# Edge keys by rounding, rounds on GpSimd, features turned ahead of the keys, and a basis schedule two parts later

## The chip, the cores and the metric

The kernel runs on one core of a Trainium2 chip. The metric is device microseconds (us) for one execution, median of several runs. All times below are us unless marked ns.

## The reference

Two graph layers over 625 nodes with 512 features each and 20,625 edges (`src`, `dst`, and a type of 0 or 1):

- Layer 0: `xw = x @ W.T`; with `deg` the number of edges into a node and `dinv = deg ** -0.5`, `h = dinv * (A @ (dinv * xw)) + b`, where `A` counts the edges between two nodes, the node itself included. Then batch norm over the nodes, gelu, `+ x`, and layer norm of `x + h`.
- Layer 1: two passes of a gated relational layer. `w[r] = sum_b att[r, b] * basis[b]` for two relations and 30 bases of 512x512; a message is `sigmoid(x[col] . gate_w[r]) * x[col] @ w[r]`, summed over the edges of type `r` into a node, plus `x @ root + bias`. Relu after the first pass, then `layernorm(x + out)`.

The two times 30 bases are 63 MB of float32 that must be read from memory.

## The kernel before

**Basis stream.** The bases are read in 64 parts of 1 MB, numbered 0 to 63, into a ring of four buffers (`basis_ring`, L397) by the SyncE queue. Part n is issued when part n-4 has been used by TensorE (`basis_used`). A part is used by 16 matmuls of 128x512 (L515); four parts sum up in one PSUM bank, and eight parts make one block of `w`. `basis_upto(n)` in TensorE's program uses the parts up to n, two at a time, and is called at fixed places.

**Edge counts.** The counts of edges between nodes, for each type, are built in `B` from 27 groups of six columns of 128 sorted edges. For a group, VectorE writes two one-hot tiles (`oh_src` and `oh_key`, L1088), TensorE multiplies them into PSUM (L596), and VectorE adds two windows of 16 nodes to `B` at an offset that it reads into a register (`window_at`, L1071, `add_window`, L1081), two groups behind. Ahead of the loop, the edges are turned by TensorE and the keys computed on VectorE. The number of further rounds (none, if every window is narrow enough) is computed by `rounds()` at group 12 and read into a register behind the loop, as are the last four window offsets.

**Beside the loop**, TensorE turns `x` (five transposes of four blocks) and `W` (four), computes `xw` in 20 steps (L563), and uses basis parts. VectorE merges the first eight parts at group 13 (`w_merge`) and writes their low halves at group 15 (`w_low`).

**Behind the loop**: the sums of the two types give `AT` (L1155, some of them turned to float by ScalarE, L846), TensorE computes `deg` (25 matmuls of two columns, L619), GpSimd the inverse root, both scale `xw` to `z`, and TensorE aggregates in four steps `f` (L639), with the counts turned to `BB` in between (L651). GpSimd issues 16 transfers of `root1` here (L455). After the gelu, TensorE turns the result back (L677), and all that follows hangs on that.

The order is written out by hand for each engine. TensorE's basis schedule in the stretch that matters is: `basis_upto(min(3 * g // 4 - 1, 17))` in group g; `basis_upto(19)` ahead of `deg`; 21 behind it; 23 after the first aggregation; 25, 27, 27 after f = 1, 2, 3; 31 ahead of the transposes of L677.

Of the kernel before, what the change touches and what calls it, by code (L numbers as in the profile page):

```python
# [38 lines left out]
P = 128  # L39
N = 625  # L40
# [18 lines left out]
MAXW = -(-N // W)  # L59
# [16 lines left out]
SWAPPED = [i ^ 1 for i in range(32)]  # L76


def gnn_block(nc, x, src, dst, etype, W0, b0, gamma, beta,
# [28 lines left out]
    with ctx:  # L108
# [50 lines left out]
        gmm = sb("gmm", [1, 4, NW], F32)  # L159
        base_i = sb("base_i", [1, NW], I32)  # L160
        spans = sb("spans", [1, MAXW], F32)
# [27 lines left out]
        edges_in, att_in = sem("edges_in"), sem("att_in")  # L189
# [44 lines left out]
        uses, releaser = {}, []  # L234

# [4 lines left out]
        for a in range(3):  # L240
            use(("edge", a), "dve")
        use("minmax", "dve")

        use("base", "dve")
        turned = [("xT", 0), ("xT", 1)] + [("w0T", k) for k in range(KC)] + [("xT", c) for c in range(2, NC)]
        use("att", "dve")
        for name in turned:
            use(name, "act")
# [101 lines left out]
        FIRST_IN = 23  # L350
# [20 lines left out]
        def edge_rows(eng, a, v):  # L371

            whole = E // (2 * P)
            eng.dma_start(rows_i[0:whole, a], v[0:whole * 2 * P].rearrange("(t h e) -> t h e", h=2, e=P)) \
                .then_inc(edges_in, 16)
            eng.dma_start(rows_i[whole:ROWS, a].rearrange("t h e -> t (h e)")[:, 0:E - whole * 2 * P],
                          v[whole * 2 * P:E].rearrange("(t e) -> t e", t=1)).then_inc(edges_in, 16)
# [5 lines left out]
        def _(sp):  # L383
            sp.wait_ge(rows_set, 3)
            edge_rows(sp, 1, dst)
# [28 lines left out]
        def _(pool):  # L414
# [20 lines left out]

            pool.wait_ge(consts, 5)
            pool.wait_ge(vec_in, 16 * 6)
# [53 lines left out]
        def _(pe):  # L491
# [38 lines left out]
            pe.wait_ge(rows_ready, 1)  # L530
            for a in range(3):
                wait_free(pe, ("edge", a))
                for h in range(2):
                    last[0] = nc.tensor.transpose(bank(("edge", a))[:, h * ROWS:(h + 1) * ROWS], rows_f[:, a, h, :],
                                                  ident[0:ROWS, 0:ROWS])
                done()
            pe.wait_ge(minmax_ready, 1)
# [3 lines left out]
            done()  # L541
            def turn(i):
# [13 lines left out]
            def xw_part(i):  # L556
# [3 lines left out]
                pe.wait_ge(in_turned, 3 + k if c == 0 else 1 + KC + c)  # L560
# [9 lines left out]
            done()  # L570
            pe.wait_ge(att_in, 16 * 2)
            pe.wait_ge(spread_ready, SUB)
# [14 lines left out]
            for i in range(FIRST_TURNS):  # L587
                turn(i)
            for g in range(NG):
# [39 lines left out]
            basis_upto(21)  # L629
# [149 lines left out]
        def _(act):  # L779
            act.wait_ge(rows_set, 3)  # L780
            edge_rows(act, 0, src)
            edge_rows(act, 2, etype)
# [34 lines left out]

            act.wait_ge(consts, 4)
            counts = B[:].rearrange("p s t n -> p (s t n)").bitcast(F32)
            link(nc.scalar.activation(counts, ones_f[0:PC, 0:1].broadcast_to(list(counts.shape)), ACT.Copy, scale=0.0))  # L820
# [132 lines left out]
        def _(dve):  # L953
# [15 lines left out]
            for q in range(SUB):  # L969
                v.tensor_copy(spread[:, q * P:(q + 1) * P].rearrange("p (b k) -> p b k", k=KB),  # L970
                              ident[0:NB, bases(q)].unsqueeze(2).broadcast_to([NB, BG, KB])).then_inc(spread_ready, 1)
            dve.wait_ge(edges_in, 16 * 6)
            link(v.tensor_copy(rows_f[:], rows_i[:]))
# [368 lines left out]
```

## Time and profile before

| what | value |
|---|---|
| runs | 312.93, 314.32, 317.32 us; median 314.32 |
| profiled execution, own time | 314.59 us |
| its span, first to last instruction | 312.7 us |
| mean granted TensorE clock | 0.960 of full |
| TensorE / VectorE / ScalarE / GpSimd busy | 88% / 51% / 29% / 12% |
| read from memory | 72.05 MB |

The span is the time between the first and the last instruction of the profiled execution; the own time is what that execution took as a whole.

### The profile page before, as it was taken

The page shows a single profiled execution, that of the slowest core. Times are in us where ns is not written, and L with a number is a line of the kernel's source. Part 1 is how long each engine was busy: PE and PEld are TensorE (multiplying, and loading weights), DVE is VectorE, ACT ScalarE, POOL GpSimd, SP SyncE. Part 2 cuts the span into 40 slices and gives each one's busy share as a digit, 9 for nine tenths or more (in the row PEclk, how much of TensorE's full clock was granted, in tenths as well). Part 3 has the DMA queues.
Part 4 walks back from the last instruction along what each step waited for, and adds up shares of the span by engine and source line. Part 5 has one row for each costly group of instructions (what it writes and reads, how often), then busy time and mean ns, then how long its engine had stood idle before and what let it go on. Part 6 is the DMA issues. An engine that isn't in the chain of part 4 may idle for free.

```text
span 312.7 us, 4598 instructions
## 1 busy us (share of the span) xinstructions
PE 276.0 (88%) x1687; PEld 180.8 (58%) x1687; DVE 160.3 (51%) x362; ACT 89.5 (29%) x140; POOL 38.3 (12%) x73
## 2 busy tenths in 40 slices
PE   1589958989799977679999999999997999999991
PEld 1573413433566643237765656677774878787770
DVE  3888888884656856855221241342434225334443
ACT  5160220201436876551352104112212242100000
POOL 2001000000292106500000000000005500011111
PEclk9999986999779999779999999999999999999997
DMA  6998992999989999958994897976002400001112
GB/s 164 231 418 326 353 410 80 415 375 369 364 259 307 413 398 426 371 183 299 388 379 171 366 343 283 419 286 265 21 1 52 118 0 0 0 2 33 33 33 66
DMA packets 12802, 73.63 MB, mean 235 GB/s; under 512 B 2000, under 2 KB 2243, under 8 KB 4588
## 3 DMA queue, kind: packets, MB, share of 16 engines
q1 hardware_dynamic: 11330, 70.82, 60.7%
q0 software_dynamic: 1104, 2.36, 2.9%
q8 instruction: 13, 0.21, 0.3%
q10 hardware_dynamic: 346, 0.17, 0.2%
q14 instruction: 9, 0.07, 0.1%
HBM read 72.05 MB, written 1.28 MB: 235 GB/s over the span
## 4 chain that ended last, share of the span: by engine, by line
PE 62%; DVE 16%; DMA 8%; issue 7%; DVEq 3%; ACT 1%; POOL 1%; ACTq 0%; POOLq 0%
PE psW L515 15%; PE psM L496 9%; PE psM L497 8%; PE psM L498 8%; PE psM L753 7%; DMA basis_ring<-in_L_gnn_basis_dram 7%; PE psM L773 6%; DVE B L1081 4%; DVEq L1071 2%; PE psM L563 2%; DVE oh_key L1088 2%; PE psE L596 2%; DVE oh_src L1088 2%; DMA rows_i<-in_edge_type_dram 1%; PE psM L639 1%
## 5 line engine op out<-in xcount | busy, mean ns | idle before, releaser
L515 PE MATMUL psW<-basis_ring,S 128*32 128x512 f32 x512 | 67.9, 646 | 6.3 <-DVEq L1057 3.7
L1267 DVE SCALAR_TENSOR_TENSOR zg<-psM,gate,zg 125x512 fp32r<-125x512 f32 x20 | 15.0, 751 | 56.9 <-ACT zg L929 56.9
L515 PEld LDWEIGHTS psW<-basis_ring,S 128*32 128x32 f32 x512 | 13.5, 114 | 41.2 <-issue 27.4
L496 PE MATMUL psM<-w,hlT 128*125 128x512 f32 x80 | 32.4, 405 | 0.1
L498 PE MATMUL psM<-w,hlT 128*125 128x512 f32 x80 | 31.7, 396 | 0.0
L497 PE MATMUL psM<-w,hlT 128*125 128x512 f32 x80 | 31.7, 396 | 0.0
L929 ACT ACTIVATE zg<-psM,gate 125x512 fp32r<-125x512 f32 x20 | 13.8, 688 | 46.3 <-PE psM L498 45.9
L596 PEld LDWEIGHTS psE<-oh_key,oh_src 128*125 128x125 f16 x162 | 13.9, 143 | 22.4 <-issue 17.3
L753 PEld LDWEIGHTS psM<-BB,zg 125*128 125x128 f32 x160 | 23.1, 188 | 3.4 <-issue 2.5
L753 PE MATMUL psM<-BB,zg 125*128 125x320 f32 (+1 forms) x160 | 24.1, 309 | 0.0
L773 PE MATMUL psM<-zg,BB 125*125 125x512 f32 x100 | 24.0, 394 | 0.0
L1081 DVE TENSOR_TENSOR B<-B,psE 125x160 f32 x54 | 17.5, 324 | 11.1 <-issue 6.6
L596 PE MATMUL psE<-oh_key,oh_src 128*125 128x160 f16 x162 | 17.0, 245 | 6.9 <-DVE B L1081 6.8
L563 PE MATMUL psM<-w0T,xT 128*125 128x512 f32 x40 | 21.7, 634 | 0.0
L773 PEld LDWEIGHTS psM<-zg,BB 125*125 125x125 f32 x100 | 18.6, 186 | 4.7
L480 POOL DMA_DIRECT2D root_raw<-in_L_gnn_root_dram x16 | 7.9, 501 | 106.8 <-DVE hlT L1297 106.8
L496 PEld LDWEIGHTS psM<-w,hlT 128*125 128x125 f32 x80 | 14.8, 185 | 9.0 <-issue 2.5
L1088 DVE TENSOR_TENSOR oh_key<-iota_f,key_pairs 128x960 f16<-128x960 f16 x27 | 17.7, 654 | 0.3
L498 PEld LDWEIGHTS psM<-w,hlT 128*125 128x125 f32 x80 | 14.8, 185 | 3.8
L497 PEld LDWEIGHTS psM<-w,hlT 128*125 128x125 f32 x80 | 14.8, 185 | 3.4
L1067 DVE TENSOR_TENSOR w<-w_both,w 128x512 fp32r<-128x512 f32 x16 | 13.1, 861 | 7.1 <-ACT w L816 6.5
L800 ACT ACTIVATE w_half<-psW,mask_h 128x512 f32<-128x512 f32 x16 | 10.1, 679 | 20.0 <-PE psW L515 20.0
(154 smaller groups left out, 381.0 us busy)
## 6 DMA issues: line engine op xcount, KB each, us to landing
basis_ring<-in_L_gnn_basis_dram SPq DMA_DIRECT2D x64, 1024.0 KB, 7.3
root_raw<-in_L_gnn_root_dram POOLq DMA_DIRECT2D x32, 64.0 KB, 3.6
xs<-in_x_dram SPq DMA_DIRECT2D x1, 1120.0 KB
out_dram<-xs SPq DMA_DIRECT2D x5, 224.0 KB
w_raw<-in_L_gnn_W_dram SPq DMA_DIRECT2D x4, 256.0 KB, 9.6
bias_b<-in_L_gnn_bias_dram POOLq DMA_DIRECT2D x1, 250.0 KB, 3.5
xs<-in_x_dram SPq DMA_DIRECT2D x1, 130.0 KB
out_dram<-xs SPq DMA_DIRECT2D x5, 26.0 KB
```

The source lines that it names most:

```text
L496: nc.tensor.matmul(o, l_hi, r_hi, start=start, stop=False)
L497: nc.tensor.matmul(o, l_hi, r_lo, start=False, stop=False)
L498: last[0] = nc.tensor.matmul(o, l_lo, r_hi, start=False, stop=stop)
L515: m = nc.tensor.matmul(psW[32 * j:32 * j + 32, cc % 2, :], S[:, cc % 2, cc // CH, q].rearrange("p k r -> p (k r)"), ring[:, n % RING, j, : ...
L563: last[0] = nc.tensor.matmul(bank(("xw", c))[0:PC, :], xT[:, k, n], w0T[:, k], start=(k == 0), stop=(k == KC - 1))
L596: nc.tensor.matmul(psE[0:PC, g % 2, at:at + KEYS], oh_src[:, g % 3, j * P:j * P + PC], oh_key[:, t % OH, :], start=(j % SG == 0), stop=(j ...
L753: last[0] = nc.tensor.matmul(bank(("h", f, h))[:, 0:n], zg[:, i, d, r, f * P:(f + 1) * P], BB[:, at:at + n], start=(d + r + i == 0), stop= ...
L773: last[0] = nc.tensor.matmul(bank(("out", c))[0:PC, :], BB[:, at:at + PC], zg[:, i, d, r, :], start=False, stop=(d == NC - 1 and r + i == 2))
L929: nc.scalar.activation(zg[:, 0, c, r, :], bank(("Z", L, c, r))[0:PC, :], ACT.Copy, scale=gate[:, L, c, r:r + 1]).then_inc(zg_hi, 1)
L1081: v.tensor_tensor(to, to, psE[0:PC, g % 2, h * KEYS:(h + 1) * KEYS] .rearrange("p (c t w) -> p c t w", c=NC, t=R), ALU.add).then_inc(win_a ...
L1088: return v.tensor_tensor(out, pair.unsqueeze(1).broadcast_to(shape), pairs[:, first:first + n].unsqueeze(2).broadcast_to(shape), ALU.is_equal)
L1267: link(v.scalar_tensor_tensor(out=zg[:, 1, c, r, :], in0=bank(("Z", L, c, r))[0:PC, :], scalar=gate[:, L, c, r:r + 1], in1=zg[:, 0, c, r, ...
```

## The change

- The keys: the chunk of a source (`src // 125`) is found by scaling, adding and subtracting a large number, instead of four comparisons; copies into `edgeT` and `base_b` are left out, VectorE reads PSUM instead; the type and chunk terms are scaled by 1/1024, so that one fused instruction brings the penalty for edges beyond a window.
- The edges: three semaphores instead of one. VectorE casts only `dst`; ScalarE casts `src` and the types and copies the turned `dst`. Clearing `B` moves from ScalarE to GpSimd. TensorE turns `dst` first, then the minima and maxima, then the other two.
- `rounds()` goes from VectorE at group 12 to GpSimd ahead of the loop, in 11 small linked instructions.
- All five turns of `x` come ahead of the loop (two of them ahead of the `att` matmuls), the four of `W` at groups 2 and 3; `xw` comes one group earlier.
- `S` is built in four instructions instead of eight and a memset.
- The first merge is at group 17 instead of 13, the low halves at 19 instead of 15.
- The registers of the last four windows and of the rounds are read between the two sums of groups 23 to 26 and 14, instead of behind the loop.
- The basis schedule: `7 * g // 10 - 2` in group g (so up to part 15 in the loop); 17 inside `deg`, behind its tenth matmul; 19 behind the vectors; 21 after the first aggregation; 23, 27, 27 after f = 1, 2, 3; 31 as before.

```diff
-        turned = [("xT", 0), ("xT", 1)] + [("w0T", k) for k in range(KC)] + [("xT", c) for c in range(2, NC)]
+        turned = [("xT", c) for c in range(NC)] + [("w0T", k) for k in range(KC)]
-        FIRST_IN = 23
+        FIRST_IN = 21
-        PARTS_IN = 17
-        FIRST_TURNS = 3
-        TURN_AT = {0: (3,), 1: (4, 5), 2: (6, 7), 3: (8,)}
-        ROUNDS_AT = 12
-        MERGE_AT = {13: 0}
-        LOW_AT = {15: 0}
+        TURN_AT = {2: (NC, NC + 1), 3: (NC + 2, NC + 3)}
+        MERGE_AT = {17: 0}
+        MORE_AT = 14
+        LOW_AT = {19: 0}
...
+            counts = B[:].rearrange("p s t n -> p (s t n)").bitcast(F32)
+            nc.gpsimd.memset(counts, 0.0).then_inc(b_clear, 1)
             pool.wait_ge(consts, 5)
+            pool.wait_ge(base_ready, 1)
+            link(nc.gpsimd.tensor_tensor(gmm[0:1, 2, :], gmm[0:1, 1, :], gmm[0:1, 0, :], ALU.subtract))
+            link(nc.gpsimd.tensor_scalar(gmm[0:1, 2, :], gmm[0:1, 2, :], -(W - 1) / 2.0, 1.0 / W, ALU.add, ALU.mult))
+            link(nc.gpsimd.tensor_scalar(gmm[0:1, 2, :], gmm[0:1, 2, :], ROUNDING, ROUNDING, ALU.add, ALU.subtract))
+            n = NW
+            while n > 1:
+                link(nc.gpsimd.tensor_tensor(gmm[0:1, 2, 0:n // 2], gmm[0:1, 2, 0:n // 2], gmm[0:1, 2, n - n // 2:n], ALU.add))
+                n -= n // 2
+            link(nc.gpsimd.tensor_scalar(more_f[:], gmm[0:1, 2, 0:1], float(N // W), None, ALU.min))
+            nc.gpsimd.tensor_copy(more_i[:], more_f[:]).then_inc(rounds_ready, 1)
...
+            for i in range(AHEAD_OF_ATT):
+                turn(i)
             pe.wait_ge(att_in, 16 * 2)
...
-                xw_upto(3 * (g - 2) // 4)
-                basis_upto(min(3 * g // 4 - 1, PARTS_IN))
+                xw_upto(3 * (g - 1) // 4)
+                basis_upto(7 * g // 10 - 2)
...
-            basis_upto(19)
             wait_free(pe, "deg")
...
+                if s == AT_ORDER[1]:
+                    basis_upto(17)
...
-            basis_upto(21)
+            basis_upto(19)
...
+            for a, arrived in ((0, src_in), (2, etype_in)):
+                act.wait_ge(arrived, 16 * 2)
+                nc.scalar.activation(rows_f[:, a], rows_i[:, a], ACT.Copy).then_inc(side_rows, 1)
+            wait_full(act, "dst")
+            link(nc.scalar.activation(edgeT[:, 1, :], bank("dst")[:, 0:T], ACT.Copy))
...
-            link(v.tensor_scalar(chunk[:], edgeT[:, 0, :], float(PC), None, ALU.is_ge))
-            for c in range(2, NC):
-                link(v.scalar_tensor_tensor(out=chunk[:], in0=edgeT[:, 0, :], scalar=float(c * PC), in1=chunk[:],
-                                            op0=ALU.is_ge, op1=ALU.add))
+            link(v.tensor_scalar(chunk[:], bank("src")[:, 0:T], -float(PC // 2), 1.0 / PC, ALU.add, ALU.mult))
+            link(v.tensor_scalar(chunk[:], chunk[:], ROUNDING, ROUNDING, ALU.add, ALU.subtract))
...
                 for i, w in enumerate(range(2 * (g - 2), 2 * (g - 1)) if g >= 2 else ()):
                     add_window(w, at[i])
-                if g == ROUNDS_AT:
-                    rounds()
+                    if i == 0 and g == MORE_AT:
+                        dve.wait_ge(rounds_ready, 1)
+                        more = nc.values_load(more_i[0:1, 0:1], engines=[mybir.EngineType.DVE], min_val=0, max_val=N // W)
+                    if i == 0 and g >= NG - 4:
+                        late.append(window_at(NW - NG + g))
...
-            more = nc.values_load(more_i[0:1, 0:1], engines=[mybir.EngineType.DVE], min_val=0, max_val=N // W)
-            at = [window_at(w) for w in range(NW - 4, NW)]
```

## Rows read from the trace of the kernel before

**Rows 1.** The page: busy time by engine; DMA share in 40 slices of 7.8 us

```profile
PE 276.0 (88%) x1687; PEld 180.8 (58%) x1687; DVE 160.3 (51%) x362; ACT 89.5 (29%) x140; POOL 38.3 (12%) x73
...
DMA  6998992999989999958994897976002400001112
```

**Rows 2.** Chain that ended last, 90 to 120 us: start, us, what

```profile
95.63 12.10 DMA basis_ring<-in_L_gnn_basis_dram
...
108.90 8.77 DMA basis_ring<-in_L_gnn_basis_dram
...
118.78 0.65 PE psM L677 x4
```

**Rows 3.** Issues of parts 12, 20 and 31, each with its time to landing

```profile
L397 SPq DMA_DIRECT2D basis_ring<-in_L_gnn_basis_dram x1: 328/328/328, 52.6 to 52.6; - x1
DMA to landing us min/median/max: 4.8/4.8/4.8
...
L397 SPq DMA_DIRECT2D basis_ring<-in_L_gnn_basis_dram x1: 328/328/328, 72.4 to 72.4; - x1
DMA to landing us min/median/max: 8.7/8.7/8.7
...
L397 SPq DMA_DIRECT2D basis_ring<-in_L_gnn_basis_dram x1: 327/327/327, 108.9 to 108.9; - x1
DMA to landing us min/median/max: 8.8/8.8/8.8
```

**Rows 4.** Busy time in three windows; last three columns: granted clock, DMA share, GB/s

```profile
76.00:78.00 2.00, 2.00 (x8) 0.53 (x10) 0.97 (x3) 0.30 (x1) 0.00 (x0) 1.00 0.97 410
...
86.00:88.00 2.00, 2.00 (x12) 0.39 (x8) 2.00 (x3) 2.00 (x4) 2.00 (x3) 0.50 0.50 201
88.00:90.00 2.00, 2.00 (x12) 0.71 (x5) 2.00 (x4) 0.15 (x1) 2.00 (x6) 0.59 0.77 209
```

**Rows 5.** Timeline, 0 to 22 us: start, us, engine line operation

```profile
6.14 0.56 DVE L973 CAST rows_f<-rows_i 81x768 f32<-81x768 int32 x1 [2.28 <-DMA rows_i<-in_edge_type_dram]
...
12.36 1.86 PE L575 MATMUL psM<-att_t,w_half 30*128 30x4 f32 x8 [2.01 <-DMA att_t<-in_L_gnn_att_dram]
...
14.13 0.55 DVE L1088 TENSOR_TENSOR oh_src<-iota_f,place_pairs 128x756 f16<-128x756 f16 x1
...
15.27 1.12 DVE L1022 TENSOR_TENSOR S<-mask_k,psM 128x64 f32<-128x64 f32 x8
...
16.72 1.01 PE L596 MATMUL psE<-oh_key,oh_src 128*125 128x160 f16 x6
...
16.90 0.55 DVE L1088 TENSOR_TENSOR oh_src<-iota_f,place_pairs 128x756 f16<-128x756 f16 x1
```

**Rows 6.** Timeline of VectorE: the rounds' first instruction, and what follows their last

```profile
39.96 0.20 DVE L1030 TENSOR_TENSOR gmm<-gmm 1x54 f32<-1x54 f32 x1
...
41.08 0.55 DVE L1088 TENSOR_TENSOR oh_src<-iota_f,place_pairs 128x756 f16<-128x756 f16 x1
```

**Rows 7.** Chain that ended last, end of the loop: sums and register loads

```profile
73.31 0.32 DVE B L1081
...
73.97 0.30 DVEq L1071
...
74.30 0.19 DVEq L1071
...
76.60 0.33 DVE B L1081
...
77.06 0.34 DVE B L1081
...
77.59 0.33 DVE B L1081
```

**Rows 8.** Timeline of TensorE behind the loop: `deg`, then parts 20 and 21

```profile
80.40 3.15 PE L619 MATMUL psM<-ones_r,AT 125*125 125x2 f32 x25 [0.69 <-ACT AT L846]
...
85.72 3.64 PE L515 MATMUL psW<-basis_ring,S 128*32 128x512 f32 x16 [1.65 <-DVEq L1057]
```

More of the change, by code:

```diff
@@ L234, in gnn_block @@
         uses, releaser = {}, []
+        AHEAD_OF_ATT = 2
         def use(name, by):
@@ L238, in use @@
             releaser.append(by)
-        for a in range(3):
-            use(("edge", a), "dve")
+        use("dst", "act")
         use("minmax", "dve")
+        use("src", "dve")
+        use("etype", "dve")
         use("base", "dve")
-        turned = [("xT", 0), ("xT", 1)] + [("w0T", k) for k in range(KC)] + [("xT", c) for c in range(2, NC)]
+        turned = [("xT", c) for c in range(NC)] + [("w0T", k) for k in range(KC)]
+        for name in turned[:AHEAD_OF_ATT]:
+            use(name, "act")
         use("att", "dve")
-        for name in turned:
+        for name in turned[AHEAD_OF_ATT:]:
             use(name, "act")
@@ L384, in _ @@
             sp.wait_ge(rows_set, 3)
-            edge_rows(sp, 1, dst)
+            edge_rows(sp, 1, dst, dst_in)
             for p in (slice(0, WIDE), slice(WIDE, PC)):
@@ L529, in _, with edges_turned @@
             pe.wait_ge(consts, 4)
-            pe.wait_ge(rows_ready, 1)
-            for a in range(3):
-                wait_free(pe, ("edge", a))
+            def edges_turned(name, a):
+                wait_free(pe, name)
                 for h in range(2):
-                    last[0] = nc.tensor.transpose(bank(("edge", a))[:, h * ROWS:(h + 1) * ROWS], rows_f[:, a, h, :],
+                    last[0] = nc.tensor.transpose(bank(name)[:, h:T:2], rows_f[:, a, h, :],
                                                   ident[0:ROWS, 0:ROWS])
                 done()
+            pe.wait_ge(rows_ready, 1)
+            edges_turned("dst", 1)
             pe.wait_ge(minmax_ready, 1)
@@ L585, in xw_upto @@
                 steps_done[0] = max(steps_done[0], n)
-            for i in range(FIRST_TURNS):
+            for i in range(AHEAD_OF_ATT, NC):
                 turn(i)
@@ L977, in _ @@
             last.then_inc(minmax_ready, 1)
-            for a in range(3):
-                wait_full(dve, ("edge", a))
-                to, ps = (ap.rearrange(how, h=2) for ap, how in ((edgeT[:, a, :], "p (t h) -> p h t"),
-                                                                 (bank(("edge", a))[:, 0:T], "p (h t) -> p h t")))
-                link(v.tensor_copy(to, ps) if a < 2 else
-                     v.tensor_scalar(to, ps, 0.0, float(W), ALU.not_equal, ALU.mult))
-                dve.sem_inc(free_dve, 1)
             wait_full(dve, "minmax")
@@ L1019, in build_S @@
                 att = bank("att")[:, 0:2 * R * SUB].rearrange("p (q l r) -> p l q r", q=SUB, l=2)
+                shape = [P, 2, SUB, KB]
                 for i, r in itertools.product(range(2), range(R)):
-                    for l in range(2):
-                        last = v.tensor_tensor(S[:, i, l, :, :, r], mask_k[:].unsqueeze(1).broadcast_to([P, SUB, KB]),
-                                               att[:, l, :, (i + r) % R].unsqueeze(2).broadcast_to([P, SUB, KB]), ALU.mult)
+                    last = v.tensor_tensor(S[:, i, :, :, :, r], mask_k[:].unsqueeze(1).unsqueeze(1).broadcast_to(shape),
+                                           att[:, :, :, (i + r) % R].unsqueeze(3).broadcast_to(shape), ALU.mult)
                 link(last)
                 dve.sem_inc(free_dve, 1)
-                link(v.memset(S[0:own(SUB - 1) * KB, :, :, SUB - 1], 0.0))
                 dve.sem_inc(ident_in, 1)
-            def rounds():
-                link(v.tensor_tensor(gmm[0:1, 2, :], gmm[0:1, 1, :], gmm[0:1, 0, :], ALU.subtract))
-                link(v.tensor_reduce(gmm[0:1, 3, 0:1], gmm[0:1, 2, :], AX.X, ALU.max))
-                link(v.tensor_scalar(spans[:], iota_f[0:1, 1:MAXW + 1], float(W), gmm[0:1, 3, 0:1], ALU.mult, ALU.is_le))
-                link(v.tensor_reduce(more_f[:], spans[:], AX.X, ALU.add))
-                link(v.tensor_copy(more_i[:], more_f[:]))
             def w_merge(pp):
@@ L1089, in one_hots @@
                                        pairs[:, first:first + n].unsqueeze(2).broadcast_to(shape), ALU.is_equal)
+            late = []
             for g in range(NG):
```

79 lines of the change are left out of this document (49 added, 30 removed).

## The prediction

> **What bounds the kernel now.** I read the page first. TensorE is busy for 88% of the span, but the DMA slices are full as well from the start to about 215 us [rows 1]: two resources are near their limit, and the busy shares alone don't say which one a given stretch hangs on. The change touches nothing behind L677 (the transposes after the gelu), so the question is which wait ends last ahead of it. The chain of waits answers it: it runs through the transfer of a basis part from 95.63 for 12.10 us, and again from 108.90 for 8.77 us, and then straight into L677 at 118.78 [rows 2]. The start of L677 therefore hangs on the landing of part 31, not on VectorE's loop. Behind L677 the same code runs in the same order, so I take it that whatever L677 moves by, the end moves by.
>
> The issues then show what limits the landing of part 31. The SyncE queue issues parts in order, each when the part four before it has been used. On an idle queue a part lands after 4.8 us (part 12, 52.6) [rows 3]. With others in front it takes 8 to 12 us: part 20 (72.4) lands at 81.1, part 31 (108.9) at 117.7 [rows 3]. At full speed the queue moves 410 GB/s [rows 4], so a part of 1.05 MB costs 2.56. Between the landings of parts 20 and 31 lie 36.6 us for 11 parts, of which 28.1 are the parts themselves. The other 8.5 are the 16 transfers of `root1`, which share the engines, and a gap: at 86 to 90 the DMA share is 0.50 and 0.77, which is 1.0 + 0.5 = 1.5 us not used [rows 4]. So from part 20 on the queue runs almost without a break, and the landing of part 31 is the landing of part 20 plus a nearly fixed time.
>
> **The change part by part.** First the loop, where it should save time.
>
> Start. Ahead of the keys VectorE casts one array instead of three, waits for `dst` only, and drops several linked instructions of some 0.3 each; first one-hots start at 14.13 now [rows 5], and I expect 11 to 12. But group 1 waits for `S`, and `S` for the `att` matmuls, which start at 12.36 when their data land and take 1.86 [rows 5]. Nothing in the change brings that transfer forward. `S` is then built from 14.2, in about 0.9 instead of 1.12 and a memset, and group 1 starts at 15.2 instead of 16.90 [rows 5]: 1.7 gained. TensorE still has three turns between `att` and the matmuls of group 0, which stay at 16.72 and take 1.01 [rows 5]; VectorE wants their sum two groups on, at 15.2 + 2 x 1.14 (14.13 to 15.27 is one pair of one-hots [rows 5]) = 17.5, and waits some 0.4. I take 1.2. The bounds: 1.7 if TensorE keeps up; 0.3 if `x` lands so late that its first two turns hold up `att` behind them on TensorE (no row shows its landing). The extra work on ScalarE (three small copies) and GpSimd (clearing `B`, 11 small instructions) ends long before anything needs it; VectorE needs the cleared `B` only at its first sum, and the rounds at group 14. Without that cover the rounds would cost VectorE a wait at group 14, with all later groups behind it.
>
> Rounds. Their five instructions on VectorE go: 39.96 to 41.08 is 1.1 [rows 6], and a little of TensorE's starvation behind them, 0.2. The merges move, with the same instructions; TensorE starves at group 17 instead of 13, which costs nothing as VectorE sets the pace there.
>
> Registers. Behind the loop the next to last sums wait for five register reads: 73.31 to 76.60 instead of the usual 0.53 between two sums of different groups (77.06 to 77.59) [rows 7]. That saves 2.8. One read is 0.30 plus 0.19 and gaps, 0.62 in all (3.1 for five). Between two sums it starts beside the first one and lets the second start 0.72 later instead of 0.46 (76.60 to 77.06) [rows 7]: 0.26 each, 1.3 for five. Bounds: 0.16 and 0.62 each.
>
> Sum: 1.2 + 1.1 + 0.2 + 2.8 - 1.3 = 4.0 us. `deg` starts at 76.4 instead of 80.40 [rows 8]. TensorE has fewer parts to use in the loop and should be free by then.
>
> The rule for the register read speaks against this part. The Trainium skill, page "DMA: Bandwidth & Descriptors", section "Latency and other measured facts", gives about 600 ns as the floor of a `tensor_load`. The trace agrees with that for the whole read (0.62), but not for the load alone (0.30). By the rule as it stands, nothing of it would be hidden, and five reads would cost 3.1; that is a rival below.
>
> Now the basis schedule. Parts 16 and 17 were used in the loop; now they stand inside `deg`, behind its tenth matmul. 10 of 25 matmuls of a stretch of 3.15 [rows 8] take 1.3, so they start at 77.7. Two parts took 3.64 at a granted clock of 0.50 [rows 4, 8], so 1.8 at full clock and 0.9 each: part 16 is used up at 78.6. Only then is part 20 issued, on a queue that has just run dry (parts 18 and 19 follow the use of 14 and 15, near 72), and it lands at 78.6 + 4.8 = 83.4. Before it landed at 81.1. So here the queue is 2.3 us later, although the loop is 4.0 earlier. The steps behind (19, 21, 23 instead of 21, 23, 25) are also one pair behind, but their parts are used early enough to keep the queue full: 22 and 23 are issued near 83, `root1` near 85, 24 and 25 near 91. With that work outstanding the gap of 1.5 at 86 to 90 is filled. Part 31 lands at 83.4 + 36.6 - 1.5 = 118.5 if all of the gap is filled, and at 120.0 if none is: 0.8 to 2.3 later than now. I take 1.3, since part of what looked like a gap is latency that stays.
>
> TensorE's side of `deg` costs nothing more: `deg` is 1.8 longer by the parts in it, but the 3.64 of parts 20 and 21 and the 1.65 of waiting ahead of them [rows 8] leave the path to the first aggregation.
>
> Where VectorE's and TensorE's 4 us go, then, is into longer waits for basis parts, at f = 2 (parts 26 and 27, now used there in a row with 24 and 25) and ahead of L677.
>
> Sum: the profiled execution had 314.59 us, 1.9 more than its span, and 0.27 more than the median of 314.32. 314.32 + 1.3 = 315.6.
>
> **The rivals.**
> (a) The queue is not the limit, and the gain of the loop reaches L677. For it: parts could land closer together than now, since `root1` comes at another point against them; the 8.5 us that they lose now is the largest unknown in my sum. Against it: the chain of waits names the transfers twice [rows 2], and the ring allows four parts ahead, no more. The compute side alone would start L677 about 3.4 earlier (4.0, less part of the time by which the last gelu is held up by four parts in a row ahead of f = 3). It gives 314.3 - 3.4 = 310.9.
> (b) Slower: TensorE has nothing to do for one or two us ahead of `deg`, and then matmuls of two columns. In the trace its granted clock is at 0.50 in 86 to 88, behind just such a stretch (a wait, `deg`, and a wait of 1.65) [rows 4, 8]. If it falls about 5 us earlier against the work, parts 16 and 17 take 1.8 each. Part 20 lands 0.9 later; if besides the start has gained 0.3 and not 1.2, another 0.9; and if the gap isn't filled, 2.3 instead of 1.3. Together 4.1: 318.4. It decides when part 20 lands after 84.5.
> (c) The register reads hide nothing (the rule above): the loop ends 5 x 0.36 = 1.8 later than in my sum, and so does part 20: 317.4.
> (d) The start doesn't gain at all, as `att` or `x` lands later: 1.2 more, 316.8. This is inside the range.
>
> **How the numbers follow.** Forecast, the queue sets L677 and lands 0 to 3 later: 0.50. (a) 0.27; (b) 0.12; (c) and (d) together 0.06; 0.05 for what I haven't seen. The range leaves out the ends of (a) and (b): from 310.9, the whole price of (a), to 318.6, that of (b). 2% is 6.3 us, which is about what a measurement of this kernel can tell from no change (its runs lie 4.4 us apart). Neither (a) nor (b) reaches it. Faster by over 2% needs the whole gain of 4.0, and 2.3 more; slower needs (b) and further lost clock behind it. I give 0.07 to each side, one more hundredth to slower.
>
> **What would show it right or wrong.** Right: `deg` starts at 75.5 to 77.5; no register reads behind the last groups; part 20 is issued at 78 to 80 and lands at 83 to 85; parts 20 to 31 land within 35 to 37 us; the chain of waits still goes through a basis transfer into L677, which starts at 119 to 121; TensorE waits longer for basis parts between 100 and 120 than it does now. Wrong: L677 starts before 117; the chain ahead of it goes through the gelu or VectorE's statistics instead of a transfer; `deg` starts after 79 (the loop's terms fail); parts 24 to 27 land without the delay from `root1`; or the end moves by something else than L677 does, as TensorE's granted clock falls at other places behind it.

## The result, and the profile after

The changed kernel takes 318.94 us (median of 4 runs, 316.86 to 321.30), the kernel before 315.82 us beside it (4 runs, 312.93 to 317.56). The ratio is 1.013, with a 95% interval of 1.008 to 1.019: slower by a little over one per cent, and outside the range that I gave by 0.3 us. My forecast of 315.6 was built on 314.32 for the kernel before, so 1.5 of the 3.3 us between 315.6 and 318.94 lie in that base (it measured 315.82 here, and 313.70 to 314.43 in three later sets of runs) and not in the change. The profiled execution of the changed kernel took 317.14 us with a span of 315.3.

The page reads almost as before [rows 1]: TensorE 88%, VectorE a little less, GpSimd 5.8 us more.

```profile
PE 278.3 (88%) x1687; PEld 183.3 (58%) x1687; DVE 159.1 (50%) x345; ACT 87.6 (28%) x142; POOL 44.1 (14%) x85
...
DMA  6994999397889999987994977977101400001112
```

The chain of waits (the work that ended last, each piece with what released it) runs from the end of the loop to the transposes behind the gelu (L707 now). It has the same two transfers in it as before [rows 2]. Each row is start, duration, what.

```profile
76.44 0.60 ACT xw L868
77.03 0.62 ACT AT L882
...
77.79 1.22 PE psM L646 x10
79.02 2.42 PE psW L533 x16
81.44 3.24 PE psM L646 x15
84.68 0.53 PE psM L655 x4
85.20 3.57 PE psW L533 x16
88.78 3.84 PE psM L669 x20
...
100.73 1.90 PE psW L533 x16
...
102.64 9.29 DMA basis_ring<-in_L_gnn_basis_dram
...
111.98 1.11 PE psW L533 x8
...
113.11 8.77 DMA basis_ring<-in_L_gnn_basis_dram
...
121.92 1.07 PE psW L533 x8
122.99 0.65 PE psM L707 x4
```

The transposes start at 122.99 instead of 118.78: 4.2 later, with a transfer of a basis part straight ahead of them as before. The first transfer in the chain is part 27. It is issued when part 23 has been used, at 102.64 instead of 95.63 [rows 2]. That is 7.0 later, of which its transfer gives back 2.8 (9.29 instead of 12.10); the last step, part 31, takes 8.77 in both.

Between 77.79 and 102.64 no transfer stands in the chain: it is TensorE's own order of work, with a short piece on ScalarE and VectorE at 93.5 to 96.4. In the kernel before it is the same, in the same chain as [rows 2] and [rows 7]:

```profile
80.40 3.17 PE psM L619 x25
...
85.72 3.64 PE psW L515 x16
89.36 3.24 PE psM L639 x20
92.60 1.11 PE psM L661 x10
93.72 1.90 PE psW L515 x16
```

Behind the first aggregation both kernels stand level. A pair of parts starts at 93.65 in the kernel before and at 93.66 in the changed one. But before it is the pair 22 and 23, and now it is 20 and 21; the pair 22 and 23 comes behind the next aggregation, at 100.66. That is the 7.0 us. The 2.6 us by which the loop ends earlier have gone by then into parts 16 to 19, which now all stand behind it.

The issues on the SyncE queue, here of parts 20 and 31, give the other end of that stretch:

```profile
L401 SPq DMA_DIRECT2D basis_ring<-in_L_gnn_basis_dram x1: 327/327/327, 80.1 to 80.1; - x1
...
DMA to landing us min/median/max: 4.8/4.8/4.8
...
L401 SPq DMA_DIRECT2D basis_ring<-in_L_gnn_basis_dram x1: 327/327/327, 113.1 to 113.1; - x1
...
DMA to landing us min/median/max: 8.8/8.8/8.8
```

Part 20 lands at 84.9 (81.1 before [rows 3]) and part 31 at 121.9: 37.0 between them, where 36.6 lay before. Part 20 isn't waited for in either kernel: it is used from 85.72 before and from 93.66 now, 4.6 and 8.8 us behind its landing.

TensorE around `deg` shows what happens in between (start, duration, operation; in brackets the idle time ahead of it and what ended that):

```profile
77.79 1.22 PE L646 MATMUL psM<-ones_r,AT 125*125 125x2 f32 x10 [1.39 <-ACT AT L882]
78.94 2.50 PE L533 MATMUL psW<-basis_ring,S 128*32 128x512 f32 x16
81.37 3.31 PE L646 MATMUL psM<-ones_r,AT 125*125 125x2 f32 x15
...
85.13 3.64 PE L533 MATMUL psW<-basis_ring,S 128*32 128x512 f32 x16
```

Parts 16 and 17 take 2.50, 15 of the `deg` matmuls 3.31, parts 18 and 19 3.64. The windows of the same stretch (granted clock, DMA share and GB/s last) say why:

```profile
78.00:80.00 2.00, 2.00 (x22) 1.34 (x25) 1.20 (x2) 0.87 (x2) 0.00 (x0) 1.00 0.89 377
80.00:82.00 2.00, 2.00 (x13) 0.63 (x4) 0.00 (x0) 0.00 (x0) 0.00 (x0) 0.54 0.49 111
82.00:84.00 2.00, 2.00 (x11) 2.00 (x11) 0.00 (x0) 0.00 (x0) 0.00 (x0) 0.50 1.03 418
...
86.00:88.00 2.00, 2.00 (x16) 0.38 (x8) 1.68 (x2) 1.79 (x4) 1.92 (x3) 0.50 0.59 246
```

The mean granted clock is 0.54 in 80 to 82 and 0.50, the 1.2 GHz level, from then on: it fell inside `deg`. And the queue is still not full: its share is 0.49 at 80 to 82 and 0.59 at 86 to 88. The gap that I wanted filled has moved, and there are two.

### The profile page after: what moved, and what is told of

Read it like the earlier page. It is cut to its first block, busy times and chain, and to the rows that moved or that the text cites. A ratio compares the mean times of both kernels' runs of the same rounds, so it can differ in the third digit from the quotient of the medians.

```text
span 315.3 us, 4596 instructions
## 1 busy us (share of the span) xinstructions
PE 278.3 (88%) x1687; PEld 183.3 (58%) x1687; DVE 159.1 (50%) x345; ACT 87.6 (28%) x142; POOL 44.1 (14%) x85
## 4 chain that ended last, share of the span: by engine, by line
PE 67%; DVE 13%; DMA 8%; issue 6%; DVEq 3%; ACT 1%; POOL 1%; SPq 0%; POOLq 0%; ACTq 0%
PE psW L533 14%; PE psM L514 9%; PE psM L516 8%; PE psM L515 8%; PE psM L783 8%; PE psM L803 6%; DMA basis_ring<-in_L_gnn_basis_dram 6%; DVE B L1106 4%; DMA xs<-in_x_dram 3%; PE psM L588 2%; PE psM L669 2%; DVE oh_key L1113 2%; DVEq L1096 2%; PE psE L623 2%; PE psM L574 1%
## 5 line engine op out<-in xcount | busy, mean ns | idle before, releaser
L533 PE MATMUL psW<-basis_ring,S 128*32 128x512 f32 x512 | 66.5, 636 | 7.0 <-DMA basis_ring<-in_L_gnn_basis_dram 4.8
L846 ACT ACTIVATE w<-w_both 128x512 fp32r<-128x512 f32 x16 | 12.9, 847 | 12.5 <-DVE w_both L1073 11.7
```

The lines of the kernel that those rows point to most:

```text
L533: m = nc.tensor.matmul(psW[32 * j:32 * j + 32, cc % 2, :], S[:, cc % 2, cc // CH, q].rearrange("p k r -> p (k r)"), ring[:, n % RING, j, : ...
```

## The experiments

Twelve kernels ran. Absolute medians differ from one set of runs to the next, so each verdict is the ratio to the kernel before, measured beside it, with its 95% interval. The ratios near one per cent have overlapping intervals; what tells those apart is the place of the events in the trace. I collect both here; times are in us, "part 23 used" is the issue of part 27, and the last column is the start of the transposes behind the gelu, by TensorE's timeline (the chain has it 0.07 later). Places are good to 0.1 us and come from one profiled execution of each kernel.

```
kernel                     ratio to before        part 20  part 23  part 31  transposes
                                                  lands    used     lands    start
before                     1                      81.1     95.6     117.7    118.7
after                      1.013 (1.008 to 1.019)  84.9    102.6    121.9    122.9
e1 old basis order         0.989 (0.984 to 0.994)  75.9     93.7    114.6    115.6
e2 new basis order alone   1.037 (1.031 to 1.043)  96.3    113.8    131.6    132.6
e3 four parts before deg   1.007 (1.003 to 1.010)  84.0     97.6    119.0    120.0
e4 four parts inside deg   1.011 (1.007 to 1.015)  84.6     96.0    119.7    120.8
e5 new order, late merge   1.021 (1.013 to 1.029)  89.2    106.5    126.0    127.0
e6 old order, early merge  0.986 (0.981 to 0.991)  76.6     94.1    113.9    115.9
e7 wide deg matmuls        1.009 (1.005 to 1.012)  84.9    101.4    120.1    121.1
e8 root1 not read          1.006 (1.002 to 1.010)  85.1    102.9    120.9    122.8
e9 22, 23 earlier          1.008 (1.003 to 1.012)  85.1     98.0    120.2    121.3
e10 e6 with wide deg       0.987 (0.984 to 0.991)  77.2     93.2    114.7    115.8
e11 e6, registers behind   0.990 (0.986 to 0.993)  76.6     93.5    114.2    115.2
e12 e6, clear on ScalarE   0.991 (0.987 to 0.995)  76.9     92.7    114.0    115.1
```

**Is it the basis schedule?** e1 is the changed kernel with the schedule of before put back, and nothing else.

```diff
-        FIRST_IN = 21
+        FIRST_IN = 23
...
-                basis_upto(7 * g // 10 - 2)
+                basis_upto(min(3 * g // 4 - 1, 17))
...
+            basis_upto(19)
...
-                if s == AT_ORDER[1]:
-                    basis_upto(17)
...
-            basis_upto(19)
-
+            basis_upto(21)
```

> The changed kernel with the basis schedule of the kernel before (up to part 17 in the loop, 19 ahead of deg, 21, 23, 25 behind it); keys, rounds, turns, merges and registers as changed. Theory Q (the transfers' queue ran dry because parts 16 to 19 are used later): part 20 is issued near 71 again, L677's transposes start at 116 to 118.5, and the time is 311 to 314, faster than the kernel before by 0.5 to 3. Rival C (the granted clock that falls inside deg is the cause, whatever the schedule): it still falls, the time stays at 317 or more. Rival L (the new loop and keys are slower): 317 or more, as nothing of them is taken back.

Measured: 310.63 us, ratio 0.989. `deg` starts at 78.12, no earlier than in the changed kernel, but parts 16 and 17 have been used in the loop, so part 20 is issued at 71.2 and lands at 75.9, 9.0 earlier, and the transposes start 7.3 earlier. The only difference between a kernel slower than before and one faster than before is this schedule. It is the cause of the loss.

e2 is the opposite: the kernel before with the new schedule alone (the same lines the other way round).

> The kernel before with the changed basis schedule alone. Theory Q: its loop ends about 2.6 later than that of the changed kernel, so part 20 is issued at 82 to 83, the transposes behind the gelu start at 124 to 126, and the time is 319 to 322, slower than the changed kernel. Rival C: as slow as the changed kernel only if the clock falls inside deg. Rival L: as the kernel before, 313 to 315.

Measured: 326.25 us, ratio 1.037, more than I expected. The reason is a collision that the changed kernel doesn't have. VectorE's timeline at the merge of before (group 13):

```profile
50.48 0.75 DVE L1049 SCALAR_TENSOR_TENSOR w_both<-psW,mask_h,w_half 128x512 f32<-128x512 f32 x1 [3.63 <-PE psW L515]
```

The merge needs parts 6 and 7, which the new schedule uses later, so VectorE stands still for 3.63 and the loop with it. (`deg` starts at 88.35, 6.8 later than in e5 below, so this wait isn't all of it; I didn't follow the rest.) Here the edit says more than the question asked. e5 therefore moves the merges along with the schedule:

```diff
-        MERGE_AT = {13: 0}
-        LOW_AT = {15: 0}
+        MERGE_AT = {17: 0}
+        LOW_AT = {19: 0}
```

> The kernel before with the changed basis schedule and the first merge at group 17 and its low halves at 19, as the changed kernel has them. Theory Q: VectorE no longer waits 3.6 us at group 13 for parts 6 and 7; deg starts near 81, part 20 is issued near 83 and lands near 88, the transposes behind the gelu start 36 to 38 later, near 125, and the time is 318.5 to 322. Rival M (the second pair of basis parts costs nothing by itself, and the 12 us of the run with the schedule alone came from the merge): 313 to 316, as the kernel before.

Measured: 321.23 us, ratio 1.021 (1.013 to 1.029). Part 20 lands at 89.2 instead of 81.1, and the transposes start 8.3 later. So the schedule by itself costs about 2%, and the changed kernel, at 1.013, has the loop's savings against it (the two intervals overlap). The later merge isn't an improvement by itself; it is what the later schedule needs.

**Where must the four late parts stand?** e3 uses parts 16 to 19 behind the loop, ahead of `deg`; e4 uses all four inside `deg`. Behind that both use the parts where the kernel before does (21, then 23 at `FIRST_IN`).

```diff
-        FIRST_IN = 21      # both
+        FIRST_IN = 23
...
+            basis_upto(19)      # e3: ahead of deg
...
-                if s == AT_ORDER[1]:      # e3: nothing inside deg
-                    basis_upto(17)
...
-                    basis_upto(17)      # e4: inside deg
+                    basis_upto(19)
...
-            basis_upto(19)      # both
-
+            basis_upto(21)
```

> The changed kernel, up to part 15 in the loop as changed, but parts 16 to 19 all used behind the loop ahead of deg, then 21, 23, 25 as in the kernel before. Theory Q: part 20 is issued near 77.3 instead of 80.1 and 22 near 79 instead of 87, so the transposes start 2 to 3.5 earlier than in the changed kernel although deg starts 2 later: 313.5 to 316. Rival C: deg's matmuls are in one stretch again; the clock falls at about 83 as in the kernel before: near 315. Rival L: 317 or more.

> The changed kernel with parts 18 and 19 used inside deg, right behind 16 and 17, then 21, 23, 25. Theory Q: part 20 is issued at 80.1 as in the changed kernel, 22 near 83 instead of 87.1, deg ends 2 to 3 later; the transposes start 1 to 2.5 earlier than in the changed kernel: 315 to 317.5. Rival C: the clock falls inside deg as now, and deg is longer: 317 to 319.

Measured: 1.007 and 1.011. Part 20 is issued at 77.7 and 79.9 and lands at 84.0 and 84.6, so the transposes come at 120.0 and 120.8. Both gain 2 to 3 us on the changed kernel's 122.9 and neither comes near e1's 115.6. e3's 316.59 us is 0.6 above what I had expected at most. What e1 has and e3 doesn't is the old schedule inside the loop, which has parts 16 and 17 in it (and the earlier parts two or three groups sooner). So of the 7.3 us by which the transposes differ between e1 and the changed kernel, 4.4 belong to the schedule inside the loop and 2.9 to the order behind it. In e3 `deg` starts at 82.35, and TensorE waits 2.01 for part 19 ahead of it; in e1, with the two parts used beside VectorE's loop, it starts at 78.12.

**Is it the gaps, the clock, or `root1`?** e7 tries to take the fall of the clock out of the changed kernel: the `deg` matmuls write 100 equal columns instead of 2, with the same count and the same result.

```diff
-                    last[0] = nc.tensor.matmul(bank("deg")[0:PC, 2 * c:2 * c + 2], AT[:, s, c * PC:(c + 1) * PC],
-                                               ones_r[:, 0:2], start=(s == AT_ORDER[0] and c == 0),
+                    last[0] = nc.tensor.matmul(bank("deg")[0:PC, 100 * c:100 * c + 100], AT[:, s, c * PC:(c + 1) * PC],
+                                               ones_r[:, 0:100], start=(s == AT_ORDER[0] and c == 0),
...
-            link(v.tensor_copy(deg[:], bank("deg")[0:PC, 0:2 * NC:2]))
+            link(v.tensor_copy(deg[:], bank("deg")[0:PC, 0:100 * NC:100]))
```

> The changed kernel; the 25 matmuls of deg stream 100 equal columns instead of 2. The weight load takes 0.12 of each matmul either way. Rival C (the granted clock that falls inside deg makes most of the 4 us): the clock stays at full through deg, parts 16 to 19 take 1.85 a pair, the transposes start 3 to 4 earlier and the time is 313.5 to 315.5. Theory Q: the clock accounts for the smaller share, 0.6 of the landing of part 20 and some 3 of the issue of part 22; if it stays up the transposes start 1 to 2 earlier, 315.5 to 317.5; if it falls nonetheless, 317 to 321 as now.

Its windows and TensorE's timeline:

```profile
80.00:82.00 2.00, 2.00 (x22) 1.16 (x15) 0.00 (x0) 0.00 (x0) 0.00 (x0) 1.00 0.47 102
82.00:84.00 2.00, 2.00 (x23) 1.32 (x26) 0.96 (x4) 0.38 (x2) 0.84 (x2) 1.00 0.96 406
```

```profile
80.88 1.84 PE L646 MATMUL psM<-ones_r,AT 125*125 125x100 f32 x15
...
82.99 1.92 PE L533 MATMUL psW<-basis_ring,S 128*32 128x512 f32 x16
```

The 15 `deg` matmuls take 1.84 instead of 3.31 and parts 18 and 19 1.92 instead of 3.64. Part 20 lands at 84.9 in both, but parts 22 and 23 are issued at 84.1 and 85.0 instead of 87.1 and 88.8. Part 31 lands at 120.1, which is 35.2 behind part 20 instead of 37.0. So the clock inside `deg` is worth 1.8 us of the 4.2. By the chain the gain is TensorE's: its first aggregation starts at 86.73 instead of 88.70, and part 23 is used at 101.4 instead of 102.6. In time the ratio goes from 1.013 to 1.009, with overlapping intervals.

e8 leaves out the transfers of `root1`: a clearing on GpSimd stands in for the 16 of them, so `root1` counts as zero in its product.

```diff
-                for j in range(JB):
-                    pool.dma_start(root1_raw[32 * j:32 * j + 32, kc],
-                                   root1.rearrange("(k c j) o -> c j k o", k=2 * KB, c=KC)[kc, j]) \
-                        .then_inc(root1_in, 16)
+                nc.gpsimd.memset(root1_raw[:, kc], 0.0).then_inc(root1_in, 1)
...
-            act.wait_ge(root1_in, 16 * KC * JB)
+            act.wait_ge(root1_in, KC)
```

> The changed kernel without the 16 transfers of root1: the tile is cleared by GpSimd instead, so root1's product is left out. It prices what these transfers take from the queue of the basis parts. Theory Q with the 8.5 us of the prediction put down to root1: parts 20 to 31 land within 29 to 32 us instead of 37, the transposes start 4 to 6 earlier, 312 to 315. Rival G (the time is lost in gaps of a queue that runs dry, root1 costs its 1 MB and no more): parts 20 to 31 take 34 to 36, the transposes start 1 to 3 earlier, 315 to 318.

Measured: 1.006 (1.002 to 1.010), part 31 35.8 behind part 20. With `root1` gone entirely only 1.2 us come back at part 31, and at the transposes 0.1, because part 31 is used at a lower clock in this profile (1.91 us instead of 1.07). I had laid a large part of 8.5 us on these transfers. But 1.2 isn't their price on the queue. Part 25 lands at 102.3 in e8 and at 107.0 in the changed kernel, 4.7 us apart; TensorE comes to it at 107.8 and 107.5, so in neither is it waited for. With `root1` gone the queue stands idle instead (its share is 0.40 at 94 to 96 and 0.54 at 102 to 104, where the changed kernel has 1.03 and 1.04), since the next parts are issued only when older ones have been used. What `root1` costs in the kernel before, where part 25 is used as it lands (101.5) and part 27's transfer in the chain takes 12.10, I didn't measure.

e9 changes one number of the changed kernel, `FIRST_IN` from 21 to 23, so that parts 22 and 23 are used right behind 20 and 21, after the first aggregation.

> The changed kernel with one number changed: 23 instead of 21 behind the first aggregation (so parts 20 to 23 are used there, 24 and 25 after f = 1, 26 and 27 after f = 2; 17 inside deg and 19 behind the vectors stay). Theory S (the delay is that of a chain: part 23 used, then the landing of part 27, then that of part 31): part 27 is issued near 97 to 98 instead of 102.6, its landing no longer waits for a late issue, the transposes behind the gelu start 2 to 4 earlier, and the time is 314.5 to 317. Theory Q as in the prediction (the queue is full from part 20 on, landings are fixed by part 20): part 31 lands at 121 to 122 as in the changed kernel and nothing is gained, 317.5 to 320.

Measured: 1.008, transposes at 121.3, 1.7 earlier. At first sight the later place of parts 22 and 23 costs 1.7. But in this profile the 15 `deg` matmuls ran at full clock (1.80) although they have two columns, so it must be read beside e7, not beside the changed kernel. Part 23 is then used 3.4 earlier (98.0 against 101.4), and part 31 lands at 120.2 against 120.1: nothing gained. TensorE now waits for the queue there, 1.13 for part 23 and 1.30 for part 25. So in the changed kernel the two limits, TensorE's order and the queue, lie close together. It also takes back a part of e7: two columns don't always let the clock fall there, so e7 shows what a full clock gives and not that the columns alone hold it.

**Is there a better kernel?** e6 is e1 with the merges back at groups 13 and 15; the other three change one thing in e6.

```diff
-        MERGE_AT = {17: 0}
+        MERGE_AT = {13: 0}
...
-        LOW_AT = {19: 0}
+        LOW_AT = {15: 0}
```

> The changed kernel with the basis schedule of the kernel before, and the merge at 13 and the low halves at 15 as well. Theory Q: parts 6 and 7 are used at group 11 in this schedule, so the place of the merge doesn't matter: 310 to 312, within 1 us of the same kernel with the merge at 17. Rival M (moving the merge is worth something by itself): over 2 us slower than that kernel.

Measured: 310.15 us, ratio 0.986 (0.981 to 0.991), the fastest here together with e10 (309.87 us, 0.987) and faster than both given kernels. Against e1 (0.989) there is no difference to be measured, so with the old schedule the place of the merge doesn't matter. Its chain of waits ahead of the transposes (L705 here) is of another kind:

```profile
113.82 1.26 ACT w_half L828 x2
115.08 0.80 ACT hf L912
...
115.93 0.72 PE psM L705 x4
```

Part 31 lands at 113.9 (TensorE waits 0.50 for it), and no transfer ends the wait ahead of the transposes: the gelu on ScalarE does, which stands in ScalarE's order behind four copies of weights. That holds for this profile only, and by under 1 us: in e1, e10, e11 and e12 the transfer of part 31 is again what TensorE waits for last ahead of the transposes, for 1.39 to 1.56 us.

e10 adds the wide `deg` matmuls of e7, e11 reads the five registers behind the loop as before, and e12 clears `B` on ScalarE instead of GpSimd:

```diff
-                    if i == 0 and g == MORE_AT:      # e11, in the loop
-                        dve.wait_ge(rounds_ready, 1)
-                        more = nc.values_load(more_i[0:1, 0:1], engines=[mybir.EngineType.DVE], min_val=0, max_val=N // W)
-                    if i == 0 and g >= NG - 4:
-                        late.append(window_at(NW - NG + g))
...
+            dve.wait_ge(rounds_ready, 1)      # e11, behind the loop
+            more = nc.values_load(more_i[0:1, 0:1], engines=[mybir.EngineType.DVE], min_val=0, max_val=N // W)
+            late = [window_at(w) for w in range(NW - 4, NW)]
...
-            nc.gpsimd.memset(counts, 0.0).then_inc(b_clear, 1)      # e12
+            link(nc.scalar.activation(counts, ones_f[0:PC, 0:1].broadcast_to(list(counts.shape)), ACT.Copy, scale=0.0))
```

> The kernel with the changed loop, the basis schedule and the merge places of the kernel before, and the 25 matmuls of deg with 100 columns. In that kernel the chain to the gelu's transposes has no transfer left, it goes through TensorE at the clock of 0.50. If the clock stays up through deg as it did in the changed kernel, parts 20 and 21 take 1.85 instead of 3.64 and the transposes start 1.5 to 3 earlier: 307.5 to 309.5. If the wait of 1.8 ahead of parts 20 and 21 lets it fall anyway: 309.5 to 311.

Measured: 0.987 against 0.986. The clock falls in any case behind TensorE's wait of 1.83 for `w_both` (0.84 in 82 to 84, 0.50 in 84 to 86), and parts 20 and 21 take 3.45. TensorE comes through part 27 0.9 earlier than in e6, but the transfer of part 31 that this issues takes longer and lands later (114.7 against 114.0), so nothing arrives at the transposes:

```profile
106.23 8.49 DMA basis_ring<-in_L_gnn_basis_dram
```

> The same kernel (changed loop, old basis schedule, old merge places) with the five register reads behind the loop, as in the kernel before. By the prediction's terms the loop's end on VectorE moves by 2.8 - 1.3 = 1.5 later: 311 to 312. Rival (TensorE sets the end of the loop): less than 0.6, about 310.5.

Measured: 0.990 (0.986 to 0.993) against 0.986 (0.981 to 0.991). The wait for the registers is back, and yet `deg` starts at 78.10 and the transposes at 115.2, as early as in e6:

```profile
74.68 0.79 DVE L1104 TENSOR_TENSOR B<-B,psE 125x160 f32 x2 [3.00 <-issue]
```

On VectorE the price came out as forecast. Its last sums end 1.3 later than in e6 (76.45 against 75.12), where I had 1.5 net. But in e6 that isn't what `deg` waits for: TensorE ends parts 18 and 19 at 78.3 and goes on to `deg` without a wait. In e11 it ends them at 76.9, since groups 23 to 26 take 1.98 us each instead of 2.26 without the reads between their sums, and then `deg` waits for `AT`. By these rows, what the reads save behind the loop they take from TensorE inside it, and the time shows no difference.

> The same kernel (changed loop, old basis schedule, old merge places) with B cleared by ScalarE behind its three small copies instead of by GpSimd. In the changed kernel two casts on VectorE took 2.8 us beside the clearing, 0.2 in the kernel before; VectorE then waited 0.4 for att. Theory G (att sets the start): the first one-hots come 1 to 1.5 earlier, S is built at the same time, 309.7 to 310.8. Rival P (the two casts cost the start): 0.5 to 1.5 faster, 308.5 to 309.6.

Measured: 0.991 (0.987 to 0.995), 311.19 us, above both expectations, though not clear of e6's interval. The start of the changed kernel and of e12 on VectorE show one thing that I hadn't foreseen and one that I had. After (VectorE, and between its rows two of TensorE):

```profile
2.44 2.79 DVE L1000 CAST ident<-ident 128x128 bf16<-128x128 f32 x1 [2.31 <-POOL BB L438]
...
10.39 1.93 PE L574 MATMUL psM<-ident,xs 125*128 125x125 f32 x8 [0.73 <-DMA xs<-in_x_dram]
12.25 1.86 PE L602 MATMUL psM<-att_t,w_half 30*128 30x4 f32 x8
...
12.51 0.55 DVE L1113 TENSOR_TENSOR oh_src<-iota_f,place_pairs 128x756 f16<-128x756 f16 x1
...
14.15 0.88 DVE L1056 TENSOR_TENSOR S<-mask_k,psM 128x128 f32<-128x128 f32 x4 [0.43 <-PE psM L602]
15.27 0.55 DVE L1113 TENSOR_TENSOR oh_src<-iota_f,place_pairs 128x756 f16<-128x756 f16 x1 [0.25 <-DVE S L1056]
```

e12:

```profile
2.45 0.23 DVE L997 CAST ident<-ident 128x128 bf16<-128x128 f32 x1 [2.31 <-POOL BB L438]
...
14.37 0.88 DVE L1053 TENSOR_TENSOR S<-mask_k,psM 128x128 f32<-128x128 f32 x4 [3.14 <-PE psM L600]
15.49 0.55 DVE L1110 TENSOR_TENSOR oh_src<-iota_f,place_pairs 128x756 f16<-128x756 f16 x1 [0.25 <-DVE S L1053]
```

In e12 the first cast takes 0.23 instead of 2.79 and the first one-hots start at 10.01 instead of 12.51. All 2.5 us of it end in a longer wait for the `att` matmuls ahead of `S` (3.14 instead of 0.43), and group 1 starts no earlier. The `att` matmuls set the start, as predicted, but not for the reason that I gave. They don't wait for `att` to land: they stand right behind the two turns of `x` that the change puts ahead of them, and those start when `x` has landed (10.39, and 10.60 in e12).

## Why the prediction was wrong

I forecast the right sign and 1.3 us; the transposes moved by 4.2. My sum had part 20 landing at 83.4 and part 31 taking 35.6 more (36.6, less 1.0 of the gap); measured are 84.9 and 37.0. So 2.9 us are missing, 1.5 in the first term and 1.4 in the second.

**"Their parts are used early enough to keep the queue full", and with it the gap of 1.5 that is filled: this is the step that failed.** I had parts 22 and 23 issued "near 83" and 24 and 25 "near 91"; they were issued at 87.1 and 88.8, and at 94.8 and 95.6. The queue was partly idle twice, at 80 to 82 and at 86 to 88, and the stretch from part 20 to part 31 got longer (37.0) where I had it 1.0 shorter. The queue waits for uses, and the uses came later for two reasons. One is the order: the pair 22 and 23 is used one aggregation later, so that part 27 is issued at 102.64 instead of 95.63. The other is the clock, which fell within `deg`; with it kept (e7) the stretch is 35.2 and the transposes are at 121.1.

**Behind this step stands a reading of the chain that was wrong.** I wrote that the start of L677 hangs on the landing of part 31, "not on VectorE's loop". The two transfers are in the chain, but ahead of them it runs back through TensorE's order and through the sums of the loop: [rows 7] are rows of the same chain. So part 31 doesn't hang on the landing of part 20, which TensorE used 4.6 us (before) and 8.8 us (after) behind its landing. It hangs on when TensorE gets through part 23, which issues part 27, and then through part 27. "Part 20 plus a nearly fixed time" fits the table as a rule of thumb: the distance is 35.0 to 37.0 in nine kernels and 37.1 to 38.7 in e1, e6, e10, e11 and e12, while the landing of part 20 ranges over 20 us. But it isn't a cause: in e4 part 20 lands as in the changed kernel (84.6 and 84.9) and part 31 2.2 earlier. The DMA slices weren't full from the start either; one of them, 47 to 55 us, stands at 2 tenths [rows 1].

**The loop, 4.0 saved, `deg` at 76.4: 1.4 too much.** `deg` starts at 77.79, 2.6 earlier than before [rows 8]. The terms on VectorE came out nearly right: its next to last pair of sums starts at 73.06 instead of 76.60 [rows 7], 3.5 earlier. Group 1 starts at 15.27 (forecast 15.2, partly by luck, as e12 shows); the rounds are gone from VectorE; a register read between two sums costs 0.29 (forecast 0.26), as these rows of VectorE show, where the second sum comes 0.75 behind the first instead of 0.46 [rows 7]:

```profile
64.99 0.32 DVE L1106 TENSOR_TENSOR B<-B,psE 125x160 f32 x1 [0.17 <-issue]
65.74 0.32 DVE L1106 TENSOR_TENSOR B<-B,psE 125x160 f32 x1 [0.43 <-DVE B L1106]
...
74.78 0.78 DVE L1106 TENSOR_TENSOR B<-B,psE 125x160 f32 x2 [0.94 <-PE psE L623]
```

What failed is that I added them up as VectorE's path and wrote that TensorE "should be free by then". The last row says it isn't: the last sums wait 0.94 for TensorE, whose matmuls of the last group stand behind parts 14 and 15 (72.23 for 1.85 in the chain). The chain then goes through TensorE's last steps of `xw` and ScalarE's copies of `xw` and `AT`, not through VectorE. e11 shows the same limit with the old schedule: 1.3 us more on VectorE, and `deg` starts at the same time. In the changed kernel itself I didn't try it.

**Part 20 on a dry queue, lands 4.8 behind its issue: right.** Issued at 80.1, landed at 84.9. It is issued 2.3 behind the start of `deg`, where I had 2.2, so nearly the whole 1.5 of this term comes from the late `deg`.

**The longer waits: half right.** TensorE waits for parts 26 and 27 at f = 2, as forecast (0.91 and 1.42, where the kernel before waited 0.06), but ahead of L677 it waits no longer than before.

**The share of `root1` in the 8.5** is open: e8 gives 1.2 at part 31, but in the changed kernel, where TensorE's order hides most of it.

**Rival (b), the clock.** It was described correctly (`deg` behind an idle spell, then two columns, a fall about 3 us earlier than in the kernel before), and given 0.12. By its own sign, part 20 landing after 84.5, it is the one that came, and its 318.4 is near the time measured. That number is luck in part: it was added up with a start that gained only 0.3 (it gained 1.6) and with 0.9 for the clock. I had laid the 0.9 on parts 16 and 17; those took 2.50 instead of 1.92, and most of the cost came later, on `deg` and on parts 18 and 19. At the transposes it made 1.8 (e7). It had to be a term of the main case: the rows of the kernel before showed the fall already [rows 4, 8], where it slows the pair 20 and 21 (3.64, in the chain); in the changed kernel it covers the rest of `deg` and a pair as well. In the profile of e9 it came later with the same `deg`, so I can't give it as a fixed price.

**Rival (a), the gain of the loop reaches the end,** didn't happen, but it does when the schedule is left alone: in e1, e6, e10, e11 and e12, with parts 16 and 17 used inside the loop, the transposes start 2.8 to 3.6 earlier than before, near the 3.4 that I had worked out. **(c)** is refuted by 0.29 for a read, half of the 0.62. **(d)** is refuted by the start.

**"Whatever L677 moves by, the end moves by": roughly.** The difference of the medians is 3.1 and of the profiled executions 2.6, against 4.2. Behind the transposes TensorE runs pairs of parts at one clock level or the other. In the profiled execution of the changed kernel this pair ran at full clock:

```profile
141.81 1.92 PE L533 MATMUL psW<-basis_ring,S 128*32 128x512 f32 x16 [2.11 <-DVEq L1082]
```

In that of the kernel before the pair at the same place took 3.51. I didn't test what decides that.

## What to carry to other kernels

When a stream of transfers with a ring of buffers is in the chain of waits, ask of every reordering when each *use* happens, for the use issues the next transfer: the schedule that leaves two parts to be used behind the loop cost 4.4 us here (e3 against e1). Follow the chain back past the transfer: what issued it, and what that waited for. Here the transfer stood at the end of a chain that TensorE's order set, and a landing that nobody waits for says little. Add up savings on the path of each engine separately, and check which one ends the stretch once the savings are in; 1.3 us on VectorE were worth nothing because TensorE ended the loop (e11 against e6). A fall of the clock that slows one pair at its present place slows more when other work is moved there.

## What the runs showed of the hardware

A cast of 128x128 on VectorE took 2.79 us while GpSimd was writing zeros to `B` (2.75 us, from 2.40), and 0.23 us in e12, where nothing was being cleared beside it (ScalarE clears `B` there from 7.01). GpSimd only writes there. The first cast took 2.56 us more of the clearing's 2.75. The Trainium skill's page "SBUF — State Buffer", section "Who interferes with whom", says that VectorE and GpSimd share a pair of ports exclusively; the trace agrees.

```profile
2.40 2.75 POOL L441 MEMSET B<- 125x3200 f32 x1
```

A part of 1.05 MB on an idle queue lands 4.8 us behind its issue (part 20: 4.6 to 5.0 in after, e1, e2, e4, e5, e7, e8 and e9); with others in front it takes 8 to 12. Where a pair's use was late, the queue's share fell to 0.49 and 0.59 over 2 us, with 0.89 to 1.03 around (after).

The same 15 matmuls of two columns took 3.31 us in one profile (after) and 1.80 in another (e9), with the same order of work up to there. The clock that this short stretch got wasn't fixed by the kernel alone.
